# A graph and expert network on one core: pieces of 7, 14, 14, 14, groups of the second convolution moved around the carry fix, places settled inside the group's statistics

## The chip, the cores and the metric

The kernel runs on one core of a Trainium2 chip. The metric is the device time of one execution in microseconds (us). Three runs of the kernel before gave 3133.04, 3133.11 and 3134.57 us, with a median of 3133.11 us.

## The reference, cut to what matters

Two layers on 6250 nodes of 256 features: a graph attention layer with two convolutions of 8 heads by 16 channels, and a mixture of 8 experts of which each node uses two. The second convolution takes, for every edge e, the edge whose number is dst[e]. As ends are below 6250, it uses only the first 6250 edges of the list, each as many times as its number occurs among the ends, so that its sums become sums over those edges, weighted with a degree.

```python
def _gat_conv(x, W, att_src, att_dst, bias, src, dst):
    xw = (x @ W).reshape(N, H, CPH)
    a_s, a_d = einsum(xw, att_src), einsum(xw, att_dst)
    src, dst = concatenate([src, loop]), concatenate([dst, loop])
    e = leaky_relu(a_s[src] + a_d[dst], 0.2)
    m = segment_max(e, dst)
    p = exp(e - m[dst])
    alpha = p / segment_sum(p, dst)[dst]
    return segment_sum(xw[src] * alpha[:, :, None], dst).reshape(N, H * CPH) + bias

h0 = _gat_conv(x, W0, as0, ad0, b0, row, col)
h1 = _gat_conv(x, W1, as1, ad1, b1, concat([row[col], loop]), concat([col[col], loop]))
out = layernorm(concatenate([h0, h1]) + x) * gamma + beta
...
x = x + gnn(layernorm(x))
x = x + ffn(layernorm(x))     # top 2 of 8 experts, softmax of their two logits, gelu between two products
```

There are 206250 edges (200000 drawn, 6250 loops), sorted by their end `dst`.

## The kernel before, in words

The five engines (PE, DVE, ACT, POOL, SP) have an instruction stream each, written out by hand, and wait for one another on named semaphores. Nodes stand in 49 tiles of 128 (`NT`), these in 7 groups of 7 (`NG`, `GRP`).

**Projections (0 to about 170 us).** Rows of x are normalised, projected with both convolutions' weights and stored in DRAM as `tables`, one row a node: 136 numbers for each convolution (128 features and 8 source scores). Destination scores go to `adt` and are scattered to the first edge of each node (`adstart`).

**The double section (`scan_piece`, L860, L1622 to L1691).** The first 6272 edges are laid out as 128 partitions of 49 edges (`J1`). These are the edges that both convolutions use, so one gathered row of the source serves both. The 49 columns go through in four pieces, `CO` = (13, 12, 12, 12), which begin at the columns `AT`. For every column POOL issues one gather of 128 rows (L860), then DVE computes scores and scans along the columns. Scans run over a fixed width, `WA` = 14, one more than the widest piece, whatever the number of columns in the piece. ACT computes the exponentials and copies the scanned states back (`copy_piece_back`, L1090) to the buffer from which they came; SP stores them, one store for each convolution (L667). There are `NS` = 3 such buffers (slots), so the gathers of piece 3 wait for the stores of piece 0, and those of the first batch for piece 1's. Ahead of piece 0, ACT needs the scores of each partition's first node, which POOL gathers (`gather_chunk_adst`, L864) behind the gathers of piece 0.

**The batches (L880, `scan_batch`, L1699 to L1730).** The other edges are 128 partitions of 1563; they go through in 51 batches (`NB`) of 31 columns, the last of 13, over the same three slots. In batches 10 to 49 PE makes 3 or 4 columns of a batch itself by products of one-hot matrices with the table (L1332, 51 matmuls a column), and POOL gathers the other 27 or 28. The last batch has views of the width `WA` too.

**The carry fix.** Each partition begins somewhere inside a node's edges, so what the partition before it had summed must be added to one row of `state`. This is done three times: a chain of small operations (`run_maxima`, `run_sums`), a gather of the row (`gather_fix_rows`, L889), its correction (`fix_maxima`, `fix_sums`), and its store (`store_fix_rows`, L895). The third, for the last batch, lies behind all batches: POOL gathers the row once all state stores have landed, and the last states of the first convolution (`last_states1`, L910) may be gathered only once the corrected row is stored. Those of the second convolution (`last_states2`, L917) depend on neither.

**Groups.** For a group, `shares(k, g)` computes how the summed edges and the node's own loop share the weight (L1992 to L1997), ACT takes exponentials (`share_exps`), and `combine(k, g)` (L2006 to L2030) adds both to the input (`halves`); k = 0 is the first convolution and k = 1 the second. The node's own rows come by SP (`own(i)`, L684) into three buffers in the order `OWN_ORDER`; own(i) waits until the group that used the buffer is combined. Groups 0 to 3 of the second convolution are combined before the loop over groups, groups 4 to 6 in its turns 1 to 3. A turn of the loop (DVE, from L2122) is:

```python
combine(0, g)
layer_stats(halves[g], g, 0, next_shares)    # next_shares: shares(0, g + 1), and shares(1, 3 + g) in turns 1 to 3
if g >= 1:
    choose(g - 1)                            # the two best experts of the group before
if 1 <= g <= 3:
    combine(1, 3 + g)
conclude(g)                                  # gamma, add x, settle(g - 1), layer_stats(X, g, 1)
```

`layer_stats` takes means and variances (L1968, L1971), adds epsilon (L1973), releases ACT for a square root, and then computes scales (L1977, L1979), which release ACT. `settle(g - 1)` (L2060 to L2082) computes the places of the group before among its experts and releases POOL, which scatters that group's rows to `placed` (`place`, L947). After the loop DVE makes the list of tiles, and the last stage multiplies 105 tiles of 128 rows with their experts' weights (from about 2360 us); the weights are loaded by SP during the loop.

Of the kernel before, what the change touches and what calls it, by code (L numbers as in the profile page):

```python
# [28 lines left out]
P = 128  # L29
# [37 lines left out]
CO = (13, 12, 12, 12)  # L67
AT = (0, 13, 25, 37)
NA = len(CO)
WA = CO[0] + 1  # L70
# [7 lines left out]
OWN_ORDER = ((1, 0), (1, 1), (1, 2), (1, 3), (0, 0), (0, 1), (1, 4), (0, 2), (1, 5), (0, 3), (1, 6), (0, 4), (0, 5), (0, 6))  # L78
# [19 lines left out]
assert (PE1 - PE0) % 2 == 0 and CL + 1 == WA and PEC < CL and 2 * HD * WA <= HL and 2 * ROWS * WA <= ROWS * L and ZT % ZJ == 0 and ZT * P == EP  # L98
# [6 lines left out]
def build(nc, x, src, dst, W0, as0, ad0, b0, W1, as1, ad1, b1, gamma, beta, Wg, bg, eW1, eb1, eW2, eb2, out):  # L105
    ctx = ExitStack()
    with ctx:
# [474 lines left out]
        def _(sp):  # L582
            with nc.allow_non_contiguous_dma(reason="small tables, once"):
# [152 lines left out]
                for g in range(NG):  # L736
                    sp.wait_ge(conv_sum_ready, g + 1)
                    for i in ((7,), (8, 9), (10, 11), (12, 13), (), (), ())[g]:
                        own(i)
# [63 lines left out]
        def _(pool):  # L803
# [120 lines left out]
            for n in range(3):  # L924
                last_states2(n)
# [3 lines left out]
            last_states2(3)  # L929
            last_states2(4, 0, 3)  # L930
            store_fix_rows(2)
            last_states2(4, 3, 5)
# [3 lines left out]
            last_states2(4, 5, GRP)  # L936
            for n in range(2, 4):
                last_states1(n)
            last_states2(5)
# [35 lines left out]
        def _(act):  # L975
# [238 lines left out]
            share_exps(1, 1)  # L1214
            fix_exps(2)
            for g in range(2, 4):
                share_exps(1, g)
            share_exps(0, 0)
            for g in range(NG):
# [9 lines left out]
                if 1 <= g <= 3:  # L1229
                    share_exps(1, 3 + g)  # L1230
# [227 lines left out]
        def _(dve):  # L1458
# [626 lines left out]
            def conclude(g):  # L2085

                gt = slice(g * GRP, (g + 1) * GRP)
                dve.wait_ge(group_normalised, g + 1)
                V.tensor_tensor(halves[g], halves[g], bc(gam[:, :].unsqueeze(1), [P, GRP, D]), ALU.mult)
                dd()  # L2090
                dve.wait_ge(x_loaded[g], 48 if g == NG - 1 else 32)
                V.tensor_tensor(X[:, gt, :], X[:, gt, :], halves[g], ALU.add).then_inc(x_gnn_ready, 1)  # L2092
                dd()
                if g >= 1:
                    settle(g - 1)
                layer_stats(X[:, gt, :], g, 1)
# [13 lines left out]
            run_sums(2)  # L2110
            fix_maxima(2)
            combine(1, 1)
            fix_sums(2)
            shares(1, 2)
            shares(1, 3)
            combine(1, 2)
            combine(1, 3)
            shares(0, 0)
            for g in range(NG):
                combine(0, g)  # L2120

                def next_shares():  # L2122
                    if g + 1 < NG:
                        shares(0, g + 1)
                    if 1 <= g <= 3:
                        shares(1, 3 + g)
# [4 lines left out]
                if 1 <= g <= 3:  # L2131
# [147 lines left out]
```

## Time and profile before

| what | value |
|---|---|
| median of three runs | 3133.11 us |
| the profiled execution's own time | 3135.7 us |
| its span, first to last instruction | 3133.9 us |
| mean granted TensorE clock | 0.843 |
| PE busy | 2195.0 us (70%) |
| DVE busy | 2285.2 us (73%) |
| ACT busy | 1642.9 us (52%) |
| POOL busy | 1915.3 us (61%) |

A row of the timeline is the start in us from the span's beginning, the duration, the engine, the line, the operation with output and inputs, the count, and in brackets the idle time of the engine ahead of it and what ended it. Busy shares are means over stages that have different limits. POOL's gathers are 0.94 us long with 0.30 us of "issue" between two, which is not counted as busy, so POOL at 61% may have no pause at all in a stage.

### The profile page before, as it was taken

How to read it: one execution, taken by the hardware profiler on the slowest of the kernel's cores; microseconds unless marked ns; L12 is line 12 of the kernel's file. 1: busy time of each engine (PE TensorE's matmuls, PEld its weight loads, DVE VectorE, ACT ScalarE, POOL GpSimd, SP SyncE). 2: the span in 40 equal slices, each digit the busy share in tenths (PEclk: the TensorE clock that was granted, in tenths of full speed). 3: DMA queues.
4: the chain of work that ended last, by engine and by line, in shares of the span. 5: the costliest groups of instructions: out<-in, count | busy, mean ns of one | idle time of the engine just before them, and what ended most of it. 6: DMA issues, size and time to landing. Idle time of an engine off the chain costs nothing.

```text
span 3133.9 us, 45939 instructions
## 1 busy us (share of the span) xinstructions
PE 2195.0 (70%) x13176; PEld 1568.0 (50%) x13177; DVE 2285.2 (73%) x4491; ACT 1642.9 (52%) x3213; POOL 1915.3 (61%) x1901
## 2 busy tenths in 40 slices
PE   3700000068999889988998898803448999999998
PEld 1500000035555445545554554403348999999997
DVE  5667765879989999988989999877864444444443
ACT  4534444567767776777777667624333333333332
POOL 4776777777777777777777777767761222222222
PEclk8855555579999999999999999955559999999999
DMA  9445449844444444445444444464772222222222
GB/s 342 128 116 141 165 166 200 153 128 127 132 160 128 127 145 146 128 128 161 130 128 141 149 128 129 151 228 156 247 250 38 36 37 37 35 37 35 37 37 31
DMA packets 215010, 401.07 MB, mean 128 GB/s; under 512 B 78620, under 2 KB 164577, under 8 KB 208337
## 3 DMA queue, kind: packets, MB, share of 16 engines
q1 hardware_dynamic: 138721, 251.00, 24.0%
q0 software_dynamic: 75024, 147.81, 20.8%
q8 instruction: 66, 1.08, 0.1%
q14 instruction: 79, 0.65, 0.1%
q10 hardware_dynamic: 1120, 0.52, 0.1%
HBM read 207.38 MB, written 191.82 MB: 127 GB/s over the span
## 4 chain that ended last, share of the span: by engine, by line
POOL 44%; PE 25%; issue 15%; DVE 7%; DMA 2%; ACT 2%; DVEq 2%; SPq 2%; POOLq 0%; ACTq 0%
POOL AR L880 42%; PE ps L1413 12%; PE ps L1419 12%; DVE group_stats L1968 1%; ACT AR L1222 1%; DMA tables<-AR 1%; SPq L604 1%; PE ps L1404 1%; POOL adstart L840 1%; DVE AR L1728 1%; DMA state<-AR 1%; DVEq L1724 1%; SPq L588 0%; DMA AR<-tables,idx 0%; DVE AR L2092 0%
## 5 line engine op out<-in xcount | busy, mean ns | idle before, releaser
L880 POOL DMA_INDIRECT AR<-tables,idx x1423 | 1360.0, 956 | 439.8 <-issue 433.1
L956 POOL DMA_INDIRECT out<-AR,idb x105 | 186.7, 1778 | 590.6 <-issue 557.0
L1332 PE MATMUL ps<-AR,eb2b 128*128 128x408 bf16 (+1 forms) x2040 | 380.6, 352 | 165.9 <-DVE eb2b L1800 165.9
L1728 DVE TENSOR_TENSOR_SCAN AR<-ps,AR 128x512 f32<-128x512 f32 (+2 forms) x459 | 484.8, 1130 | 6.4
L1113 ACT ACTIVATE ps<-AR 128x512 f32<-128x512 f32 (+1 forms) x408 | 238.3, 592 | 345.6 <-DVE AR L1728 345.6
L1121 ACT COPY AR<-AR 128x1984 f32<-128x1984 f32 (+1 forms) x102 | 401.7, 3987 | 0.0
L1413 PEld LDWEIGHTS ps<-AR 128*128 128x128 f32 x3360 | 393.1, 193 | 6.6 <-DVE AR L2182 1.3
L1413 PE MATMUL ps<-AR 128*128 128x128 f32 x3360 | 393.7, 276 | 0.9 <-DVE AR L2182 0.9
L1332 PEld LDWEIGHTS ps<-AR,eb2b 128*128 128x128 bf16 x2040 | 206.5, 104 | 336.8 <-issue 211.0
L1332 PE MATMUL ps<-AR,scores 128*128 128x408 bf16 (+1 forms) x2040 | 349.3, 332 | 19.2 <-DVE AR L1787 19.0
L1332 PE MATMUL ps<-AR,own_pair 128*128 128x408 bf16 (+1 forms) x2100 | 352.2, 327 | 0.0
L1720 DVE TENSOR_TENSOR AR<-AR,ps 128x3968 f32<-128x3968 f32 (+1 forms) x51 | 349.3, 6848 | 1.3 <-ACT AR L1100 1.3
L2182 DVE COPY AR<-AR 128x1024 f32 x210 | 151.5, 722 | 209.8 <-PE ps L1413 208.3
L1332 PEld LDWEIGHTS ps<-AR,scores 128*128 128x128 bf16 x2040 | 195.5, 99 | 168.4 <-DVE AR L1787 24.8
L1332 PEld LDWEIGHTS ps<-AR,own_pair 128*128 128x128 bf16 x2100 | 200.4, 98 | 146.5 <-issue 0.4
L1262 ACT ACTIVATE AR<-ps,bcur 128x128 f32<-128x128 f32 x424 | 121.1, 369 | 258.4 <-PE ps L1413 258.4
L1262 ACT ACTIVATE zero<-ps,bcur 128x128 f32<-128x128 f32 x416 | 118.9, 369 | 253.5 <-PE ps L1413 253.4
L1332 PE MATMUL ps<-AR,zero 128*128 128x408 bf16 x960 | 182.1, 349 | 39.6 <-DVE AR L1787 39.6
L1162 ACT ACTIVATE scores<-AR,minus_code 128x128 bf16<-128x128 f32 x680 | 202.8, 389 | 0.0
L1349 PE MATMUL ps<-ident,sml 128*128 128x128 f32 x6 | 2.4, 502 | 278.9 <-DVE sml L1868 278.9
L1419 PE MATMUL ps<-AR 128*128 x848 | 191.9, 379 | 1.3 <-DVE AR L2225 1.3
L1419 PE MATMUL ps<-AR,zero 128*128 x832 | 188.2, 379 | 0.0
(382 smaller groups left out, 3243.2 us busy)
## 6 DMA issues: line engine op xcount, KB each, us to landing
state<-AR SPq DMA_DIRECT2D x50, 2232.0 KB
AR<-tables,idx POOLq DMA_INDIRECT x1472
AR<-in_L_ffn_W SPq DMA_DIRECT2D x16, 1024.0 KB, 9.7
AR<-placed SPq DMA_DIRECT2D x105, 130.0 KB, 2.0
adstart<-zero SPq DMA_DIRECT2D x26, 496.0 KB, 13.4
AR<-adstart SPq DMA_DIRECT2D x50, 248.0 KB, 4.3
tables<-AR SPq DMA_DIRECT2D x49, 136.0 KB, 1.9
hbd<-eb2b SPq DMA_DIRECT2D x7, 896.0 KB, 4.3
```

The source lines that it names most:

```text
L880: pool.indirect_dma_start(out=G[s][:, j, 0:ROWT], out_offset=None, in_=table_rows, in_offset=bass.IndirectOffsetOnAxis(ap=idx[:, s, j:j + ...
L956: pool.indirect_dma_start(out=out, out_offset=bass.IndirectOffsetOnAxis(ap=idb[:, s, :], axis=0), in_=ys[:, s, :], in_offset=None, bounds_ ...
L1113: S.activation(decay_of(e, w).rearrange("p (c l) -> p c l", l=w), bc(R[:, e - 1, :].unsqueeze(1), [P, CH, w]), ACT.Exp).then_inc(decays_re ...
L1121: last = S.copy(G[s][:, 0:n, a:z], TS[:, a:z, 1:n + 1].rearrange("p f j -> p j f"))
L1162: last = S.activation(onehot[c][:, a, :], column_codes[:, slot(b), c * P:(c + 1) * P], ACT.Abs, bias=minus_code[:, a:a + 1])
L1262: last = S.activation(hsT[s][:, m, :], ps[2 * s + h][:, (m % 4) * P:(m % 4 + 1) * P], ACT.Gelu, bias=bcur[:, s, m:m + 1])
L1332: mm = T.matmul(ps[n % 2][:, 0:z], mark, table_parts[k][:, a * w:a * w + z], start=(a == 0 and k == 0), stop=(a == LEV - 2 and k == PARTS ...
L1413: mm = T.matmul(ps[2 * s + h][:, m * P:(m + 1) * P], w1_cur[:, k, (h * 4 + m) * P:(h * 4 + m + 1) * P], xsT[:, s, k, :], start=(k == 0), s ...
L1419: mm = T.matmul(ps[5][:, 0:D], hsT[s][:, m, :], AR[:, bass.ds(e * (MH * D) + (NEX * KD * HID + m * D), D)], start=(m == 0), stop=(m == MH ...
L1720: V.tensor_tensor(TS[:, 0:F, js].rearrange("p (h c) j -> p h c j", h=HD), rows_in[:, :, 0:F].rearrange("p j (h c) -> p h c j", h=HD), bc(W ...
L1728: V.tensor_tensor_scan(T2[:, a:z], decay_of(e, w), T2[:, a:z], 0.0, ALU.mult, ALU.add).then_inc(entry_used, 1)
L2182: V.tensor_copy(w1_cur[:, :, h * 512:(h + 1) * 512], w1s[:, bass.ds(e, 1), :, h * 512:(h + 1) * 512].rearrange("p a k h -> p (a k) h")).th ...
```

## The change

It has three parts. The pieces of the double section have 7, 14, 14 and 14 columns, so that `WA` becomes 15. On POOL, DVE, ACT and SP the second convolution's groups are reordered around the third carry fix: POOL gathers the last states of group 3 ahead of the fix row and all of group 4 ahead of the row's store, DVE computes shares(1, 2) ahead of `fix_maxima(2)`, and combines group 4 ahead of the loop instead of in turn 1; `OWN_ORDER` follows. And `settle(g - 1)` is called inside `layer_stats(X, g, 1)`, between the variances and the wait for their square roots.

```diff
-CO = (13, 12, 12, 12)
-AT = (0, 13, 25, 37)
+CO = (7, 14, 14, 14)
+AT = (0, 7, 21, 35)
 NA = len(CO)
-WA = CO[0] + 1
+WA = max(CO) + 1
...
-OWN_ORDER = ((1, 0), (1, 1), (1, 2), (1, 3), (0, 0), (0, 1), (1, 4), (0, 2), (1, 5), (0, 3), (1, 6), (0, 4), (0, 5), (0, 6))
+OWN_ORDER = ((1, 0), (1, 1), (1, 2), (1, 3), (1, 4), (0, 0), (0, 1), (0, 2), (1, 5), (0, 3), (1, 6), (0, 4), (0, 5), (0, 6))
...
-                    for i in ((7,), (8, 9), (10, 11), (12, 13), (), (), ())[g]:
+                    for i in ((7, 8), (9,), (10, 11), (12, 13), (), (), ())[g]:
                         own(i)
...
-            for n in range(3):
+            for n in range(4):
                 last_states2(n)
             for s in range(NS):
                 pool.wait_ge(batch_stored[s], stored_count(s))
             gather_fix_rows(2)
-            last_states2(3)
-            last_states2(4, 0, 3)
+            last_states2(4)
             store_fix_rows(2)
-            last_states2(4, 3, 5)
+            last_states2(5, 0, 2)
             pool.wait_ge(fix_rows_stored, 48)
             for n in range(2):
                 last_states1(n)
-            last_states2(4, 5, GRP)
+            last_states2(5, 2, GRP)
             for n in range(2, 4):
                 last_states1(n)
-            last_states2(5)
             last_states2(6)
...
             share_exps(1, 1)
+            share_exps(1, 2)
             fix_exps(2)
-            for g in range(2, 4):
-                share_exps(1, g)
+            share_exps(1, 3)
+            share_exps(1, 4)
             share_exps(0, 0)
...
-                if 1 <= g <= 3:
+                if 2 <= g <= 3:
                     share_exps(1, 3 + g)
...
                 V.tensor_tensor(X[:, gt, :], X[:, gt, :], halves[g], ALU.add).then_inc(x_gnn_ready, 1)
                 dd()
-                if g >= 1:
-                    settle(g - 1)
-                layer_stats(X[:, gt, :], g, 1)
+
+                def settle_the_last():
+                    if g >= 1:
+                        settle(g - 1)
+
+                layer_stats(X[:, gt, :], g, 1, settle_the_last)
...
             run_sums(2)
+            shares(1, 2)
             fix_maxima(2)
             combine(1, 1)
             fix_sums(2)
-            shares(1, 2)
             shares(1, 3)
             combine(1, 2)
+            shares(1, 4)
             combine(1, 3)
+            combine(1, 4)
             shares(0, 0)
...
-                    if 1 <= g <= 3:
+                    if 2 <= g <= 3:
                         shares(1, 3 + g)
...
-                if 1 <= g <= 3:
+                if 2 <= g <= 3:
                     combine(1, 3 + g)
                 conclude(g)
```

On POOL, around the fix row's gather (L889) and its store (L895), the difference reads as follows; `eb2b`, `zero` and `hT` hold last states of the second convolution, `AR` at L910 those of the first, and x7 is one group.

```order
 L917 DMA eb2b<-state,node_index 128x144 x14
 L917 DMA zero<-state,node_index 128x144 x7
+L917 DMA hT<-state,node_index 128x144 x7
 L889 DMA fix_row<-state,fix_index 128x144
-L917 DMA hT<-state,node_index 128x144 x7
-L917 DMA eb2b<-state,node_index 128x144 x3
+L917 DMA eb2b<-state,node_index 128x144 x7
 L895 DMA state<-fix_row,fix_index 206336x144
 L917 DMA eb2b<-state,node_index 128x144 x2
 L910 DMA AR<-state,node_index 128x144 x14
-L917 DMA eb2b<-state,node_index 128x144 x2
+L917 DMA eb2b<-state,node_index 128x144 x5
```

Seven gathers went ahead of the fix row's gather, and seven instead of ten stand between it and the row's store.

On DVE, at the end of what comes ahead of the loop, the combining of group 3 was followed at once by the shares of the first convolution's group 0 (L1992 with `AR`):

```order
L2023 TENSOR_TENSOR hT<-hT,share_of 128x7x128
L2023 TENSOR_TENSOR own_pair<-own_pair,share_of 128x7x128
L2028 TENSOR_TENSOR AR<-AR,hT 128x7x128
L2030 TENSOR_TENSOR AR<-AR,own_pair 128x7x128
L1992 TENSOR_TENSOR share_of<-AR,bare 128x56
L1994 TENSOR_TENSOR share_of<-share_of,own_score 128x56
```

In the change, where these lines are numbered one less:

```order
L2027 TENSOR_TENSOR AR<-AR,hT 128x7x128
L2029 TENSOR_TENSOR AR<-AR,own_pair 128x7x128
L2005 TENSOR_TENSOR share_of<-eb2b,share_of 128x56
L2010 SCALAR_TENSOR_TENSOR share_of<-share_of 128x56
L2012 RECIPROCAL share_of<-share_of 128x56
L2014 TENSOR_TENSOR share_of<-share_of 128x56
L2018 SCALAR_TENSOR_TENSOR share_of<-share_of 128x56
L2022 TENSOR_TENSOR eb2b<-eb2b,share_of 128x7x128
L2022 TENSOR_TENSOR own_pair<-own_pair,share_of 128x7x128
L2027 TENSOR_TENSOR AR<-AR,eb2b 128x7x128
L2029 TENSOR_TENSOR AR<-AR,own_pair 128x7x128
L1991 TENSOR_TENSOR share_of<-AR,bare 128x56
```

Group 4's nine instructions of `combine` now stand there, and are gone from turn 1 of the loop.

On DVE, in the second half of a turn of the loop, the places (to L2082) came ahead of the statistics:

```order
L2074 COPY AR<-nid 128x7
L2075 COPY AR<-gate_w 128x7x2
L2082 CAST ipos<-pos 128x14
L1968 BN_STATS group_stats<-AR 128x6 x7
L1971 BN_AGGR group_mv<-group_stats 128x2 x7
L1973 TENSOR_SCALAR group_mv<-group_mv 128x7
L1977 RECIPROCAL group_scale<-group_scale 128x7
```

In the change:

```order
L1972 TENSOR_SCALAR group_mv<-group_mv 128x7
L2059 TENSOR_REDUCE mask_new<-route_of 128x8
L2061 TENSOR_SCALAR gate_w<-gate_w 128x7
L2063 TENSOR_TENSOR mask_sum<-mask_sum,mask_new 128x8
L2066 RECIPROCAL gate_w<-gate_w 128x7
L2068 TENSOR_TENSOR gate_w<-gate_w 128x7
L2070 TENSOR_TENSOR route_of<-route_of,ps 128x112
L2072 TENSOR_REDUCE pos<-route_of 128x14
L2073 COPY AR<-nid 128x7
L2074 COPY AR<-gate_w 128x7x2
L2081 CAST ipos<-pos 128x14
L1976 RECIPROCAL group_scale<-group_scale 128x7
```

The ten instructions of `settle` now stand between the operation that releases ACT for the square root and the one that needs it.

## Rows read from the trace of the kernel before

**Rows 1.** The page's part 4: the chain that ended last, by engine.
```profile
POOL 44%; PE 25%; issue 15%; DVE 7%; DMA 2%; ACT 2%; DVEq 2%; SPq 2%; POOLq 0%; ACTq 0%
```

**Rows 2.** Waits over the whole span: total us, times, longest us.
```profile
POOL AR L880 <- issue: 433.1, 1421, 0.3
...
POOL AR L880 <- DMA state<-AR: 6.4, 1, 6.4
...
POOL AR L860 <- DMA state<-AR: 4.2, 1, 4.2
```

**Rows 3.** Busy time by stretch: PE, PEld, DVE, ACT, POOL, PEclk, DMA share, GB/s.
```profile
640.00:680.00 40.00, 28.33 (x151) 15.59 (x152) 30.83 (x42) 29.34 (x52) 30.25 (x33) 0.84 0.40 127
...
720.00:760.00 40.00, 37.34 (x228) 21.37 (x226) 37.73 (x46) 34.67 (x64) 30.25 (x33) 1.00 0.44 131
...
600.00:2044.00 1444.00, 1243.20 (x7140) 696.40 (x7140) 1290.90 (x1604) 1020.72 (x1694) 1092.54 (x1154) 0.94 0.44 137
```

**Rows 4.** Timeline of POOL in the double section.
```profile
171.51 0.99 POOL L860 DMA_INDIRECT AR<-tables,idx  x1 [0.30 <-issue]
...
187.83 0.94 POOL L864 DMA_INDIRECT chunk_adst<-adt,ifirst  x1 [0.30 <-issue]
...
245.43 0.94 POOL L880 DMA_INDIRECT AR<-tables,idx  x1 [6.40 <-DMA state<-AR]
```

**Rows 5.** Timeline of DVE in the double section; L1622 begins a piece.
```profile
190.98 0.38 DVE L1622 COPY ps<-same 128x208 f32<-128x208 f32 x1 [25.97 <-ACT AR L1062]
...
212.36 0.35 DVE L1622 COPY ps<-same 128x192 f32<-128x192 f32 x1
...
224.74 7.93 DVE L1685 TENSOR_TENSOR_SCAN AR<-ps,AR 128x448 f32<-128x448 f32 x8
...
233.09 0.36 DVE L1622 COPY ps<-same 128x192 f32<-128x192 f32 x1
```

**Rows 6.** Timeline of ACT: the copies of piece 1.
```profile
230.25 6.19 ACT L1090 COPY AR<-AR 128x1728 f32<-128x1728 f32 x2
```

**Rows 7.** Timeline of SP's queue: the two stores of piece 1.
```profile
236.83 0.91 SPq L667 DMA_DIRECT2D state<-AR  x2
```

**Rows 8.** Timeline of POOL around the third carry fix.
```profile
2081.50 0.98 POOL L889 DMA_INDIRECT fix_row<-state,fix_index  x1 [11.36 <-DMA state<-AR]
...
2096.26 1.01 POOL L895 DMA_INDIRECT state<-fix_row,fix_index  x1 [0.30 <-issue]
```

**Rows 9.** DMA queues from 2070 to 2082 us: packets, MB, share of 16 engines.
```profile
q1 hardware_dynamic: 2046, 4.47, 100.7%
```

**Rows 10.** Timeline of DVE from the corrected row to the loop.
```profile
2095.17 0.06 DVE L1921 MEMSET sml<- 128x1 f32 x1
...
2096.86 0.21 DVE L2006 TENSOR_TENSOR share_of<-zero,share_of 128x56 f32<-128x56 f32 x1
...
2102.95 0.22 DVE L2006 TENSOR_TENSOR share_of<-hT,share_of 128x56 f32<-128x56 f32 x1
...
2116.18 0.22 DVE L1992 TENSOR_TENSOR share_of<-AR,bare 128x56 f32<-128x56 f32 x1 [7.23 <-DMA AR<-state,node_index]
```

**Rows 11.** Timeline of DVE in the loop; L2006 with AR begins turns 3, 4, 5.
```profile
2206.68 0.21 DVE L2006 TENSOR_TENSOR share_of<-AR,share_of 128x56 f32<-128x56 f32 x1
...
2235.90 2.39 DVE L1968 BATCH_NORM_STATS2 group_stats<-AR 128x6 f32<-128x256 f32 x7
...
2239.01 0.17 DVE L1973 TENSOR_SCALAR group_mv<-group_mv 128x7 f32<-128x7 f32 x1
2239.46 0.20 DVE L1977 RECIPROCAL group_scale<-group_scale 128x7 f32<-128x7 f32 x1 [0.27 <-ACT group_scale L1209]
...
2239.82 0.21 DVE L2006 TENSOR_TENSOR share_of<-AR,share_of 128x56 f32<-128x56 f32 x1
...
2264.39 0.21 DVE L2006 TENSOR_TENSOR share_of<-AR,share_of 128x56 f32<-128x56 f32 x1
```

**Rows 12.** Timeline of POOL: the first scatter of the last group's rows.
```profile
2332.59 0.96 POOL L947 DMA_INDIRECT placed<-AR,ipos  x1 [6.14 <-DVE ipos L2082]
```

More of the change, by code:

```diff
@@ L97 @@
 assert NBLK * BLK == E and NG * GRP == NT and (NB + NA) % NS == 1 and sum(CO) == J1 and max(CO) * 2 * ROWS <= J * ROWS
-assert (PE1 - PE0) % 2 == 0 and CL + 1 == WA and PEC < CL and 2 * HD * WA <= HL and 2 * ROWS * WA <= ROWS * L and ZT % ZJ == 0 and ZT * P == EP
+assert (PE1 - PE0) % 2 == 0 and CL + 1 <= WA and PEC < CL and 2 * HD * WA <= HL and 2 * ROWS * WA <= ROWS * L and ZT % ZJ == 0 and ZT * P == EP
 def bc(ap, shape):
```

## The prediction

> **What bounds the kernel now.** I read the chain that ended last first [rows 1]: POOL 44%, PE 25%, issue 15%. "Issue" is mostly POOL's too, the 0.30 us between two gathers. The list of waits says whether POOL ever pauses [rows 2]: its 1423 gathers of the batches have 433.1 us of issue in pieces of at most 0.3 us, and one wait of 6.4 us for a store of states; the double section's have one of 4.2 us. Both are in the double section. From its first batch gather at 245.43 us [rows 4] POOL issues one every 1.25 us until about 2044 us, never waiting. The row of that stretch agrees [rows 3]: over 600 to 2044 us POOL has 1092.5 us busy and the rest is issue, while DVE is busy 1290.9 of 1444 us and PE 1243.2. So whatever starts the batches earlier arrives whole at their end. Then come two other limits: DVE waits 7.23 us for the last states of the first convolution [rows 10], and in the loop over groups DVE is nearly always busy. The last stage is PE's and is not touched.
>
> **Part 1, the pieces.** From 171.51 to 187.83 us POOL issues 13 gathers [rows 4], 1.255 us each. With 7 columns in piece 0 the gather for the first nodes' scores comes 6 x 1.255 = 7.5 us earlier, and DVE, which waits for ACT's copy of it, starts piece 0 at 190.98 - 7.5 = 183.5 us [rows 5]. A piece of 13 columns takes DVE 212.36 - 190.98 = 21.38 us, one of 12 takes 20.73 [rows 5]: 0.65 a column. The width goes from 14 to 15, so the scans of 448 elements (7.93 us) become 480, +0.57, and I add 0.1 for the narrower full-width operations. Piece 0 then takes 20.73 - 5 x 0.65 + 0.67 = 18.2 us, and those of 14 take 22.7. Piece 0 ends at 201.6 and piece 1 at 224.3.
>
> Piece 0's stores are half as large as now and start near 203 us. POOL wants their slot after 35 column gathers and 2 for scores, at 171.5 + 37 x 1.255 = 217.9, so the wait of 4.2 us goes. What is late next is piece 1's store, which now has 14 columns. ACT's copy starts 233.09 - 230.25 = 2.8 us ahead of DVE's end and takes 6.19 us for 12 columns [rows 6], 7.2 for 14: it ends at 228.6. From the end of that copy now (236.44) to POOL's restart (245.43) are 9.0 us, the stores being issued at 236.83 [rows 7]. Two more columns in two stores are 0.29 MB, 0.8 us at the 373 GB/s that the hardware queue moved when it was full [rows 9]. POOL restarts at 228.6 + 9.8 = 238.4, having been free since 171.5 + 51 x 1.255 + 0.3 = 235.8. **Gain 245.4 - 238.4 = 7.0 us.** Bounds: only the first pause goes, 3.9 us; both go, 10.0. I take the sum, since every step of it is a row of the same code. Later slots are covered: batch 1 needs piece 2's store, about 23 us after piece 1's, and asks for it after 31 gathers, 39 us.
>
> The last batch has the width 15 too: some 140 more scan elements at 7.93 / (8 x 448) = 2.2 ns. **Cost 0.3 us** (0.1 to 0.5).
>
> **Part 2, the order around the fix.** POOL stands 11.36 us ahead of the fix row's gather, waiting for the last store [rows 8]. The seven gathers moved there take 8.8 us, so the wait hides them, and 2.6 us stay. Behind the gather the seven of group 4 wait for combine(1, 0), which ends about when the fix gather goes out, and run till about 2092.5, earlier than the corrected row at 2095.17 [rows 10]. POOL now reaches the store 1.1 us after that [rows 8] and would then wait for it, so the store leaves up to 1.0 us earlier. The two gathers behind it and the fourteen of the first convolution are as many as before, as is the traffic of SP. shares(1, 2) falls into DVE's wait for the fix row and costs nothing.
>
> The Trainium skill speaks against this move. Row first: from 2070 to 2082 us the hardware queue, which carries the last store of states, is busy 100.7% [rows 9]. "DMA: Bandwidth & Descriptors", section "Queues, rings and completion order", says that each DMA engine takes turns between the queues that have work for it. By it the moved gathers, 7 x 128 x 576 B = 0.52 MB, push that store back by their own time, and the sum would be smaller by the figure of the first rival below; by the row alone, the store lands as it does now.
>
> DVE now begins combine(1, 2) at 2096.86 and combine(1, 3) at 2102.95, 6.09 us each, and then waits 7.23 us [rows 10]. The change puts combine(1, 4) there: DVE is ready at 2116.18 - 7.23 + 6.09 = 2115.0, and the data comes at 2116.2 or up to 1.0 earlier. I take **gain 0.5 us** (from 1.1 gained to 2.5 lost). If the cover were gone, combine would cost its 6.09.
>
> In the loop, turn 3 (with a group of the second convolution) takes 2239.82 - 2206.68 = 33.1 us, and turn 4 (without) 2264.39 - 2239.82 = 24.6 [rows 11]. The 8.6 us are combine, shares, and a wait for ACT's exponentials. Turn 1 becomes one of the second kind. **Gain 8.6 us** (7.5 to 9.4). Loads of own rows change their order on SP; each still leaves at least one combine ahead of its use, and costs nothing.
>
> **Part 3, settle.** Between the variances (L1973) and the scales (L1977) DVE spends 0.45 us, 0.27 of it idle for the square root [rows 11]. With settle in between, the root is ready and only an issue gap is left. ACT gets the scales by as much earlier, and nothing is added to DVE. The six turns from 1 on give **6 x 0.36 = 2.2 us** (0.27 to 0.45 each: 1.6 to 2.7). The places are known later by the statistics, 2239.01 - 2235.90 = 3.1 us. POOL waits 6.14 us for the last group's places [rows 12], which come from behind the loop and do not get later; the group before may eat 3.1 of it. Cost zero, up to 1.5 if the weights' last loads, released by that group's scatters, press on the tile loads.
>
> **The sum:** 7.0 - 0.3 + 0.5 + 8.6 + 2.2 = **18.0 us**. Against the profiled execution's own 3135.7 us (span 3133.9) that is 3117.7; it was 2.6 us above the median of 3133.1, to which the same gain gives **3115.1 us**. A measurement of this kernel can tell about 0.2%, 6.3 us, from no change.
>
> **Rivals.**
> 1. *The store is late, and the gap overfilled.* The moved gathers delay the last store by 0.52 MB / 373 GB/s = 1.4 us, and everything behind it on the way to the corrected row; combine(1, 1), in that path, stays where it is. Gain 0.5 turns into a loss of 1.4, and up to 2.5 with a slow gather: 3117 to 3118. For it: the full queue [rows 9]. Against it: the fix row's own gather then meets less traffic. It is the page's rule above that would make this so. Chance 0.15.
> 2. *The pause only moves.* Piece 1 waits for its gathers, or its larger stores take longer, and of part 1 only the 3.9 us of the first pause remain: 3118. Against it: its last gather leaves at 199 us, 4 us before DVE wants it. Chance 0.07.
> 3. *The loop is held by the scatters.* POOL scatters a group in 14 x (0.96 + 0.30) = 18 us [rows 12] in turns of 24.6, but the late places and shorter turns bunch it up. If POOL or the weights' loads hold the end, the 10.8 us of the loop shrink to 3 and less: 3123 to 3128. Against: 6.14 us of pause at the end [rows 12]. Chance 0.05.
> 4. *Slower.* In the columns that PE makes, its clock falls at times to the lower of its levels (1.2 and 2.4 GHz): granted 0.84 over 640 to 680 us, after DVE and PE had waited for each other, 1.00 over 720 to 760 [rows 3]. At full clock a matmul there takes 37.34 / 228 = 0.164 us. A batch has 3.5 columns of 51, so 29 us, against 27.5 x 1.25 = 34 us of POOL. At the lower level it is 58, 24 us over POOL. If the shifted start lines up PE's pauses so that one whole batch more runs at the lower level, the gain is gone and more; two give 3115 + 48 = 3163. It decides from one batch and a quarter, 18 + 6.3 = 24.3. For it: the clock does dip, mean 0.94. Against: nothing in that stage moves with respect to anything else. Chance 0.04, half of it slower by 0.2%.
>
>    The Trainium skill's page "TensorE: Matmul & The Clock Gate", section "HAM oscillation — how this bites in real kernels", has waits between groups of matmuls throttle the clock again; the row with 0.84 agrees.
>
> That settle brings nothing, because what ends the wait is something else, would give 3117 and is inside the range.
>
> **The numbers.** Main case 0.69 and rivals 0.15, 0.07, 0.05, 0.04. The bounds of the parts add up to 9 to 23 us of gain. The range is 3110 to 3122: 3110 is every part at its best, and 3122 is rivals 1 and 2 together with a poor part 3. Faster by over 0.2% are the main case, rivals 1 and 2 and half of 3: 0.93. Within 0.2%: 0.05. Slower: 0.02.
>
> **What would show it.** In the new profile POOL waits for stores of the double section only ahead of the first L880, for 2 to 3.5 us, and that L880 starts near 238.4 us; L860 has no such wait. The fix row's gather goes out about 7 us earlier than 2081.5, after 2 to 4 us of pause instead of 11.4. DVE's wait ahead of the first L1991 with `AR` is under 1.5 us. Turn 1 takes 24 to 25 us and turns 2 and 3 33. The waits of L1976 for ACT's root vanish in turns 1 to 6 of the second statistics. It is wrong if the first L880 starts after 241 us, if the fix row's gather leaves less than 5 us earlier, or if the last stage, from the first tile's load on, changes its length.

## The result, and the profile after

The changed kernel takes 3116.61 us (median of 6 runs, 3115.36 to 3119.34) against 3134.62 us (6 runs, 3133.04 to 3134.92): ratio 0.9946, 95% interval 0.9935 to 0.9957, 18.0 us less. The forecast was 3115.1, range 3110 to 3122. Its profiled execution took 3115.67 us with a span of 3113.9, against 3135.7 and 3133.9 before. So this pair of profiles shows 20.0 us; 1.6 of them had come about ahead of the first L860 (169.94 us, 171.51 before), where nothing was changed.

The page's part 4 of the changed kernel, the chain by engine, answers to [rows 1]. It has hardly moved:

```profile
POOL 46%; PE 25%; issue 16%; DVE 6%; DMA 3%; ACT 2%; SPq 2%; DVEq 2%; POOLq 0%; ACTq 0%
```

The list of POOL's and DVE's waits in the changed kernel (total us, times, longest us) answers to [rows 2, 8, 10]:

```profile
POOL AR L880 <- issue: 433.0, 1421, 0.3
...
POOL placed L945 <- DVE ipos L2081: 13.8, 5, 3.7
...
POOL AR L880 <- DMA state<-AR: 3.2, 1, 3.2
POOL state L895 <- DVE sml L1920: 2.6, 1, 2.6
POOL fix_row L889 <- DMA state<-AR: 2.6, 1, 2.6
```

```profile
DVE AR L1903 <- DMA fix_row<-state,fix_index: 3.1, 1, 3.1
...
DVE share_of L1991 <- DMA AR<-state,node_index: 2.1, 1, 2.1
...
DVE AR L2027 <- DMA AR<-hbd: 1.2, 1, 1.2
...
DVE group_scale L1976 <- ACT group_scale L1207: 0.5, 2, 0.3
```

Gone are the wait of L860, 8.8 of the 11.4 us ahead of the fix row's gather, and six of the eight short waits for ACT's root. Left is one wait of 3.2 us at L880. POOL's wait of 2.6 us for the corrected row (L895) is new and was expected. New as well is a wait of 2.1 us for last states of the first convolution. The prediction had only the one ahead of the loop in mind, and that one is gone: this is another.

The double section in the changed kernel, in the order DVE, ACT, SP's queue, POOL, one fence each; compare [rows 4 to 7]:

```profile
181.54 0.28 DVE L1621 COPY ps<-same 128x112 f32<-128x112 f32 x1 [17.31 <-ACT AR L1060]
```

```profile
219.43 7.12 ACT L1088 COPY AR<-AR 128x2016 f32<-128x2016 f32 x2
```

```profile
226.94 0.91 SPq L667 DMA_DIRECT2D state<-AR  x2
```

```profile
236.62 0.94 POOL L880 DMA_INDIRECT AR<-tables,idx  x1 [3.20 <-DMA state<-AR]
```

Each stretch shows what it is worth on its own. Lengths in us, all between starts of instructions in the timelines; the runs e7 to e12 are told below.

| stretch | before | changed | e6 again | e7 pieces | e8 order | e9 settle | e10 states first | e11 settle back | e12 both mends |
|---|---|---|---|---|---|---|---|---|---|
| A first L860 to first L880 | 73.92 | 66.68 | 67.16 | 66.72 | 73.84 | 73.74 | 66.86 | 67.06 | 64.15 |
| B first to last L880 | 1797.5 | 1796.6 | 1798.9 | 1796.0 | 1800.5 | 1796.4 | 1799.0 | 1796.7 | 1794.9 |
| C last L880 to the last store of states (SP) | 27.92 | 27.64 | 30.20 | 28.63 | 27.62 | 29.16 | 27.80 | 27.79 | 27.96 |
| D that store to the fix row's gather | 10.61 | 11.71 | 11.57 | 10.39 | 12.05 | 10.30 | 11.61 | 11.74 | 11.47 |
| E fix row's gather to turn 0 of the loop | 35.97 | 34.57 | 34.82 | 36.22 | 35.47 | 36.04 | 34.63 | 34.51 | 34.54 |
| F turn 0 to the last choice (first L2036, or L2035) | 205.61 | 195.88 | 196.17 | 205.70 | 196.48 | 205.09 | 193.78 | 196.55 | 193.75 |

The 20.0 us of the first pair are 1.6 ahead of A, 7.2 in A, 0.9 in B, 0.3 in C, 0.3 in D and E together, and 9.7 in F. From the last choice to the end there are 810.8 and 810.9 us.

In F one stretch went against the rest. Turn 5, from L2005 with `AR` of the one turn to that of the next, took 24.45 us before and takes 26.12 now. DVE and POOL in the changed kernel:

```profile
2243.15 0.21 DVE L2005 TENSOR_TENSOR share_of<-AR,share_of 128x56 f32<-128x56 f32 x1
...
2254.65 0.22 DVE L1991 TENSOR_TENSOR share_of<-AR,bare 128x56 f32<-128x56 f32 x1 [2.07 <-DMA AR<-state,node_index]
...
2269.27 0.21 DVE L2005 TENSOR_TENSOR share_of<-AR,share_of 128x56 f32<-128x56 f32 x1
```

```profile
2218.88 0.99 POOL L945 DMA_INDIRECT placed<-AR,ipos  x1 [2.09 <-DVE ipos L2081]
...
2238.67 0.96 POOL L945 DMA_INDIRECT placed<-AR,ipos  x1 [0.30 <-issue]
2239.93 0.99 POOL L910 DMA_INDIRECT AR<-state,node_index  x1 [0.30 <-issue]
...
2249.10 0.94 POOL L910 DMA_INDIRECT AR<-state,node_index  x1 [0.30 <-issue]
```

`shares(0, 6)` needs the last states of group 6. POOL gathers them (L910, until 2249.10) behind the 14 scatters of group 2, which it could begin only when that group's places were known, at 2218.88. In the kernel before, POOL's last gather for group 6 stood at 2264.44, and DVE wanted it at 2273.67, 9.2 us later; here these are 2249.10 and 2252.6 (2254.65 - 2.07), and the data takes 5.6:

```profile
2264.44 0.98 POOL L910 DMA_INDIRECT AR<-state,node_index  x1 [0.30 <-issue]
```

```profile
2273.67 0.26 DVE L1992 TENSOR_TENSOR share_of<-AR,bare 128x56 f32<-128x56 f32 x1
```

The margin before was therefore 9.24 - 5.55 = 3.7 us. My theory when the experiments began: the places that settle now gives 3.1 us later, and the turn that became shorter, used it up together.

### The profile page after: what moved, and what is told of

It is laid out like the page before. It is cut to its first block, busy times and chain, and to the rows that moved or that the text cites. A ratio compares the mean times of both kernels' runs of the same rounds, so it can differ in the third digit from the quotient of the medians.

```text
span 3113.9 us, 45939 instructions
## 1 busy us (share of the span) xinstructions
PE 2202.4 (71%) x13176; PEld 1572.2 (50%) x13177; DVE 2287.4 (73%) x4491; ACT 1644.8 (53%) x3213; POOL 1920.0 (62%) x1901
## 4 chain that ended last, share of the span: by engine, by line
POOL 46%; PE 25%; issue 16%; DVE 6%; DMA 3%; ACT 2%; SPq 2%; DVEq 2%; POOLq 0%; ACTq 0%
POOL AR L880 43%; PE ps L1412 12%; PE ps L1418 12%; POOL adstart L840 1%; DMA tables<-AR 1%; PE ps L1403 1%; DVE group_stats L1967 1%; ACT AR L1221 1%; DMA state<-AR 1%; SPq L604 1%; POOL placed L945 1%; SPq L588 0%; DVE AR L1684 0%; DVE AR L2091 0%; DVE AR L2088 0%
## 5 line engine op out<-in xcount | busy, mean ns | idle before, releaser
L880 POOL DMA_INDIRECT AR<-tables,idx x1423 | 1359.1, 955 | 436.5 <-issue 433.0
L1331 PE MATMUL ps<-AR,zero 128*128 128x408 bf16 x960 | 188.5, 357 | 39.0 <-DVE AR L1786 39.0
```

The lines of the kernel that those rows point to most:

```text
L880: pool.indirect_dma_start(out=G[s][:, j, 0:ROWT], out_offset=None, in_=table_rows, in_offset=bass.IndirectOffsetOnAxis(ap=idx[:, s, j:j + ...
L1331: mm = T.matmul(ps[n % 2][:, 0:z], mark, table_parts[k][:, a * w:a * w + z], start=(a == 0 and k == 0), stop=(a == LEV - 2 and k == PARTS ...
```

## The experiments

### Five runs on chips where the kernel takes 4400 us

The first five runs went to two chips on which the kernel before takes 4416.9 us (e1 to e4) and 4378.7 us (e5), not 3134. Of their expectations only the fifth allows for that.

e1, the pieces alone:

```diff
-CO = (13, 12, 12, 12)
-AT = (0, 13, 25, 37)
-WA = CO[0] + 1
+CO = (7, 14, 14, 14)
+AT = (0, 7, 21, 35)
+WA = max(CO) + 1
```

> The kernel before with the pieces of 7, 14, 14, 14 alone. My theory: the pieces are worth what the two traces show, 7.2 us at the first L880 counted from the first L860 (73.9 us before, 66.7 us expected), less 0.3 us for the wider last batch, and it all arrives: 6.5 to 7.5 us faster than before. It arrives whole because POOL never waits between that L880 and the last batch. Rival A (the pause only moves): the first L880 comes 3.9 us earlier, 3 to 4 us in the time. Rival B: the gain is eaten where POOL's stream ends, since the last store, PE's columns or DVE's scan are what the last batch waits for, and less than half of the shift at L880 is seen at the fix row's gather. The last store of states, with only three groups of gathers beside it as before, should take 10.6 us from SP's issue to POOL's restart (it took 11.7 in the changed kernel with seven more gathers beside it).

e2, the order alone: the change without this and without the move of settle.

> The kernel before with the new order around the fix alone (POOL, DVE, ACT and SP lists), pieces and settle as before. My theory: the first L880 stays at 245 us; turn 1 of the loop falls from 33.5 to 24 us (9.6) and the gap before the first shares of the first convolution gains about 1, less nothing later, as the places are not late here: 9.5 to 10.5 us faster than before. Rival A (my first rival in the prediction, the overfilled gap): the seven more gathers push the last store back by 1.4 us, the gap loses 1 to 2, and the gain is 7 to 8 us. Rival B: the wait of 2 us for the last states of group 6 comes from the shorter loop alone, not from the late places, and shows here too ahead of the sixth turn's shares: 8 us faster. By my theory that wait is under 0.5 us here.

e3, settle alone:

```diff
-                if g >= 1:
-                    settle(g - 1)
-                layer_stats(X[:, gt, :], g, 1)
+                def settle_the_last():
+                    if g >= 1:
+                        settle(g - 1)
+
+                layer_stats(X[:, gt, :], g, 1, settle_the_last)
```

> The kernel before with settle between the variances and the scales, nothing else. My theory: in the kernel before POOL has slack in the loop (turns 1 to 3 long), so the late places cost nothing and the six closed gaps are seen: 2.2 us faster (1.6 to 2.7). Rival A: something else ends the turns, 0 us. Rival B: the places 3.1 us later hold POOL back here too, a wait of about 2 us for the last states of group 6 shows, and the time is the same or up to 1 us worse.

e4, POOL's order alone: the piece of the diff around `gather_fix_rows(2)`, and nothing on DVE, ACT and SP.

> The kernel before with POOL's new order alone: the fourth group of seven gathers moved ahead of the fix row's gather, DVE, ACT and SP as before, so that turn 1 still holds group 4 of the second convolution. My theory: the moved gathers only fill a wait; 0.5 to 1.5 us faster than before, and what the new order brings comes from DVE's side, the turn made short. Rival: POOL's chain was what held the loop, and moving its gathers alone brings 5 us or more.

e5, the changed kernel with POOL's loop written in another order:

```diff
             for n in range(NG):
+                if n == 2:
+                    last_states1(n + 4)
                 place(n)
-                if n + 4 < NG:
+                if n < 2:
                     last_states1(n + 4)
```

> The changed kernel with one thing moved on POOL: the last states of the first convolution's group 6 are gathered ahead of the scatters of group 2, not behind them. My theory: in the changed kernel the sixth turn of the loop is 1.7 us longer than before the change because DVE waits 2.07 us for these states, and they are late because POOL waits 2 to 4 us for places in three turns and then scatters 18 us first. Moved ahead, they are there in time: the wait ahead of the sixth turn's shares vanishes, that turn takes 24.1 instead of 26.1 us, and the kernel takes 1.5 to 2.5 us less than the changed one (20 less than the kernel before). Rival A: the scatters of group 2, then 9 us later, make the wait move to POOL's next places and to the last group's, 0 us or up to 2 worse. Rival B: DVE's wait there is for something else, and it stays. On a chip where the kernel before takes 4417 us, as in the four runs ahead of this one, the loop is held by something else (POOL waits 9 to 18 us for places in every turn) and all three expect 0.

Measured, as ratios to the kernel before on the same chip: e1 0.9976 (0.9936 to 1.0016), e2 0.9958 (0.9920 to 0.9996), e3 0.9965 (0.9932 to 0.9998), e4 0.9962 (0.9930 to 0.9994), e5 0.9993 (0.9958 to 1.0028). The medians are 4420.4, 4403.8, 4413.2 and 4412.8 us, and 4369.1 for e5; as plain ratios 1.0008, 0.9970, 0.9991, 0.9991 and 0.9978. The intervals of e2, e3 and e4 end just below 1, but the two ways to take a ratio differ by up to 0.3%, as much as the effects, and half a width of 0.3 to 0.4% is 14 to 18 us: e1 to e5 decide nothing between their theories. e4, POOL's order alone, was not run again on another chip, so what POOL's list brings without DVE's is not known. The profile says why the five could not decide. POOL's waits in e1:

```profile
POOL AR L880 <- DMA state<-AR: 1127.4, 23, 59.7
```

Busy time from 1070 to 1080 us in e1, then in the changed kernel on the first chip (PE, PEld, DVE, ACT, POOL, PEclk, DMA share, GB/s), both in the columns that PE makes while POOL gathers:

```profile
1070.00:1080.00 10.00, 1.99 (x4) 0.31 (x3) 0.00 (x0) 0.00 (x0) 7.57 (x8) 0.50 0.39 118
```

```profile
1070.00:1080.00 10.00, 10.00 (x62) 5.74 (x61) 9.71 (x9) 8.15 (x19) 7.56 (x9) 1.00 0.25 57
```

And PE in e1, where the bracket is its idle time before the matmul:

```profile
1073.33 0.50 PE L1332 MATMUL ps<-AR,scores 128*128 128x408 bf16 x1 [1.61 <-issue]
1076.12 0.50 PE L1332 MATMUL ps<-AR,scores 128*128 128x408 bf16 x1 [2.29 <-issue]
...
1117.45 3.92 PE L1332 MATMUL ps<-AR,scores 128*128 128x408 bf16 x11 [0.20 <-issue]
```

PE issues one matmul in 1.4 to 2.8 us (once in 4.2), where the first chip makes 62 in 10 us. In this batch it begins 11 us after POOL has taken up its gathers (1040.07 us) and ends 5 us after its last one (about 1108 us). PE and POOL so work by turns: POOL waits up to 59.7 us for a slot. The batches are not POOL's alone there, and the prediction's "whatever starts the batches earlier arrives whole at their end" does not hold.

It is not PE alone. This is DVE in piece 1 of the double section in e1, while PE does nothing at all:

```profile
239.50 0.39 DVE L1622 COPY ps<-same 128x224 f32<-128x224 f32 x1
...
260.16 0.45 DVE L1664 TENSOR_TENSOR AR<-AR,ps 128x112 f32<-128x112 f32 x2 [4.75 <-issue]
...
283.65 0.39 DVE L1622 COPY ps<-same 128x224 f32<-128x224 f32 x1
```

The piece takes 44.2 us and not the 22.5 of the first chip. DVE is busy 21.52 us in both; here eleven pauses put down to "issue", 22.5 us in all, stand between its instructions, and the last of them ends as POOL makes its last gather of the section (267.86 us). POOL then waits 27.8 us for that piece's store. That is most of why stretch A is longer there, and why it changes its sign: 91.5 us in e1 with the new pieces, 87.7, 87.5 and 87.9 in e2 to e4 with the old ones. In e2 the pauses of that piece are 13.6 us and POOL's waits 4.3 and 20.2.

In the loop of e5 POOL waits 4.6 to 11.8 us for places in every turn, and DVE waits for no last states, so POOL's gathers hold nobody. Why these chips do this is open; no run tried it.

### The change again, and its three parts, at 3136 us

The sixth run was the changed kernel itself.

> The changed kernel itself, once more. If this chip runs the kernel before in 3134 us, as where the change was first measured: 18 us faster. If it runs it in 4380 to 4420 us, as the chips of the five runs ahead of this one, my theory (there PE issues one matmul in 1.4 to 2.8 us for as long as POOL gathers, so POOL and PE work by turns and the stream of batches is no longer POOL's alone) expects that the first L880 comes 3 to 4 us later than with pieces of 13, 12, 12, 12 (91.5 us from the first L860 in the run with the pieces alone, 87.5 to 87.9 in the three without them), and that the time is 5 to 15 us less than before, from the loop alone. Rival: the gain of 18 us holds wherever the kernel runs, since the loop and the double section have nothing to do with the batches.

It came to a chip with 3136.2 us for the kernel before, and the changed kernel took 3122.76 (3122.08 to 3123.30): ratio 0.9953 (0.9937 to 0.9970), 13.4 us. Stretches A and F are those of the first profile within 0.5 us. Its profiled span is 7.7 us longer (3121.6); 1.6 of that stand ahead of A and 4.9 in B and C, where the table has scatter of that size between profiles. "The gain is 18" is thus good to some 3 us, though each mechanism is good to half a microsecond. Runs e7 to e10 then went to the same chip (12), with 3137.64 us for the kernel before.

e7, the pieces alone again.

> The kernel before with the pieces of 7, 14, 14, 14 alone, once more, on a chip that runs the kernel before in 3135 us. My theory: the first L880 starts 66.7 us after the first L860 (73.9 before) and 6.5 to 7.5 us arrive in the time. Rival A (the pause only moves): 3 to 4 us. The last store of states takes 10.6 us from SP's issue to POOL's restart, as before and not 11.7 as in the changed kernel, if the seven gathers beside it are what delayed it there. On a chip that takes 4400 us: the first L880 3 to 4 us later than before, no change in the time.

3131.27 us, ratio 0.9981 (0.9972 to 0.9991), 6.4 us less. POOL in this kernel:

```profile
238.40 0.94 POOL L880 DMA_INDIRECT AR<-tables,idx  x1 [3.23 <-DMA state<-AR]
...
2073.41 0.94 POOL L889 DMA_INDIRECT fix_row<-state,fix_index  x1 [11.83 <-DMA state<-AR]
```

A is 66.72 us, 7.2 less than before; the rival with 3 to 4 us is out. D is 10.39 us, as in the two other profiles with the old order (10.61, 10.30).

e8, the order alone again.

> The kernel before with the new order around the fix alone, once more. My theory: 9.5 to 10.5 us faster than before: turn 1 of the loop 33.5 to 24 us, the gap before the loop about 1 better, and no wait above 0.5 us for the last states of group 6, since the places are not late here. Rival A (the overfilled gap): 7 to 8 us. Rival B (the shorter loop alone makes that wait of 2 us): 8 us, and the wait shows. On a chip that takes 4400 us: 5 to 15 us faster.

3127.88 us, ratio 0.9971 (0.9959 to 0.9983), 9.8 us less. POOL in this kernel, then DVE at the last shares before the loop:

```profile
2084.98 1.01 POOL L889 DMA_INDIRECT fix_row<-state,fix_index  x1 [3.18 <-DMA state<-AR]
...
2099.44 1.07 POOL L895 DMA_INDIRECT state<-fix_row,fix_index  x1 [3.74 <-DVE sml L1920]
```

```profile
2119.15 0.22 DVE L1991 TENSOR_TENSOR share_of<-AR,bare 128x56 f32<-128x56 f32 x1 [0.72 <-DMA AR<-state,node_index]
```

F is 9.1 us shorter, all of it in turn 1 (33.50 to 24.36 us). DVE still waits 0.72 us, so the gap is filled and not overfilled. But D is 12.05 us: the first rival's mechanism is real. E is half a microsecond shorter than before, which does not make up for it: D and E together are 47.5 us against 46.6, so the gap, expected about 1 us better, is 0.9 worse. By the stretches this run gains 9.1 - 0.9 = 8.2 us, which is rival A's figure (7 to 8) and not my theory's; the median of 9.8 can't decide, as the stream of batches scatters by more than the difference. There is no wait for group 6's last states, so the short turn alone does not cause it.

e9, settle alone again.

> The kernel before with settle between the variances and the scales, nothing else, once more. My theory: POOL has slack in that kernel's loop, so 2.2 us faster (1.6 to 2.7). Rival A: something else ends the turns, 0 us. Rival B: the later places cost here too, a wait of about 2 us for the last states of group 6, and 0 to 1 us slower.

3136.77 us, ratio 0.9999 (0.9989 to 1.0009): nothing. My theory missed here, and the wait of Rival B came:

```profile
2273.88 0.22 DVE L1992 TENSOR_TENSOR share_of<-AR,bare 128x56 f32<-128x56 f32 x1 [2.04 <-DMA AR<-state,node_index]
```

Turns 1 to 4 are 33.10, 32.96, 32.76 and 24.10 us, 0.4 to 0.5 less each than in e7 (33.57, 33.39, 33.13, 24.57), and turn 5 is 26.10 against 24.43. So the late places are enough by themselves, and POOL's slack in the kernel before was smaller than I took it for.

e10, the kernel of e5 again.

> The changed kernel with the last states of group 6 gathered ahead of the scatters of group 2 on POOL, once more. My theory: DVE's wait of 2.07 us ahead of the sixth turn's shares vanishes, that turn takes 24.1 and not 26.1 us, and the kernel takes 1.5 to 2.5 us less than the changed one: 20 less than the kernel before where the changed one gives 18, 15.5 where it gives 13.4 as in the run ahead of this one. Rival A: the scatters of groups 2 and on come 9 us later and hold the last places, 0 to 2 us worse than the changed one. Rival B: the wait stays.

3118.62 us, ratio 0.9942 (0.9925 to 0.9960), 19.0 us less. DVE no longer waits at these shares (L1993 in this kernel), as the missing bracket says:

```profile
2255.72 0.21 DVE L1993 TENSOR_TENSOR share_of<-AR,bare 128x56 f32<-128x56 f32 x1
```

Turn 5 takes 23.90 us, F 193.78: 2.1 to 2.4 us less than the changed kernel. No later wait of POOL for places is longer than before: 2.03 and 2.59 us ahead of the last two groups, as in the changed kernel. The expectation of 15.5 us was short: Of the 6.2 us between its profile and that of e6, 2.4 are F, and nearly all of the rest is again C and what comes ahead of A.

### Two last runs

They went to a chip (4) with 3134.45 us for the kernel before. e11 is the changed kernel with the diff of e3 undone: `settle` stands ahead of the statistics again, as in the kernel before. ("Behind the scales" in the expectation is a slip.)

> The changed kernel with settle put back behind the scales. My theory, after the run with settle alone: the move closes gaps of 0.27 us and more in every turn (2.2 us in all) and gives the same 2 us back as DVE's wait for the last states of group 6, because it makes the places 3.1 us later and POOL scatters before it gathers. Put back, turns 1 to 4 are 0.4 us longer each, the sixth turn 24.5 us without that wait, and from the loop's first turn to the last choice it takes 196.3 to 196.7 us, against 195.9 and 196.2 in the two profiles of the changed kernel: the same time within 0.5 us. Rival: the move is worth its 2.2 us and the wait comes from the shorter loop, so that the wait stays and the kernel is 2 us slower than the changed one. On a chip that takes 4400 us: no difference can be told.

3117.61 us, ratio 0.9947 (0.9933 to 0.9961): the changed kernel's own 0.9946. F is 196.55 us, within the 196.3 to 196.7 expected, and `shares(0, 6)` does not wait:

```profile
2254.56 0.25 DVE L1991 TENSOR_TENSOR share_of<-AR,bare 128x56 f32<-128x56 f32 x1
```

e12 is e10 with smaller first and larger last pieces:

```diff
-CO = (7, 14, 14, 14)
-AT = (0, 7, 21, 35)
+CO = (5, 14, 15, 15)
+AT = (0, 5, 19, 34)
```

> The changed kernel with two mends: the last states of group 6 ahead of the scatters of group 2, as in the run before, and pieces of 5, 14, 15, 15 columns (width 16). My theory of part 1: what is left there is POOL's wait of 3.2 to 3.5 us for piece 1's store; a first piece of 5 lets DVE begin 2.5 us earlier, each wider piece costs it 0.6 us, and the first L880 starts 64.0 to 64.5 us after the first L860 (66.7 to 67.2 with 7, 14, 14, 14), after a wait of 0.3 to 1.2 us. Less 0.3 us for the last batch, 2 us less than with the first mend alone: 21 us faster than the kernel before, ratio 0.9935. Rival A: the wider pieces make a later store late (a wait in batch 1 or 2), and nothing or less is gained. Rival B: POOL's stream is not what starts the batches any more, the 2.5 us do not arrive at the end. On a chip that takes 4400 us: nothing can be told.

3113.40 us (3110.96 to 3114.85), ratio 0.9933 (0.9919 to 0.9947), 21.05 us less than before. POOL now reaches the first batch without a wait for a store:

```profile
235.43 0.94 POOL L880 DMA_INDIRECT AR<-tables,idx  x1 [0.54 <-issue]
```

A is 64.15 us, inside 64.0 to 64.5, and F is 193.75. It is the fastest of all that ran. That it beats the changed kernel rests on A (2.5 us, in this one profile) and F (2.1, here and in e10); the intervals of the two ratios overlap.

## Why the prediction was right, point by point

**The double section** was right in each step. DVE begins piece 0 at 181.54 us, 11.6 us behind the first L860; the prediction had 183.5 - 171.5 = 12.0. Piece 0 takes 18.4 us (18.2 predicted), piece 1 22.5 (22.7), ACT's copy 7.1 (7.2). From its end, 226.55 us, to POOL's restart are 10.1 us (9.8). Gain 7.2 against 7.0, and 6.4 us of it in the time of e7. The last batch's 0.3 us can't be told: C is 27.6 to 29.2 us with the old width and 27.6 to 30.2 with the new one.

**The gap around the fix** came out near its sum where the new pieces ran with it (D and E: 46.58 us before, 46.28 and 46.39 in the changed kernel; 0.5 predicted), but not in e8, and a step of it was wrong. "By the row alone, the store lands as it does now" failed. With seven more gathers beside it the last store lands after 11.5 to 12.1 us (six profiles), without them after 10.3 to 10.6 (three): 1.3 us, where the rival had worked out 1.4. SP's transfers ahead of that store are the same in all of them. The delay agrees with what the Trainium skill's page "DMA: Bandwidth & Descriptors", section "Queues, rings and completion order", says, that a DMA engine takes turns between its queues. Other loads pay as well: DVE waits 0.7 to 1.6 us for `hbd` with the new order, at most 0.3 with the old.

What made good for it is E, 1.2 to 1.5 us shorter in the five profiles that have the new pieces too. Before, it ended with a wait for data [rows 10]; now it ends with DVE's own work, from the corrected row to the first shares:

```profile
2085.74 0.06 DVE L1920 MEMSET sml<- 128x1 f32 x1
...
2105.87 0.22 DVE L1991 TENSOR_TENSOR share_of<-AR,bare 128x56 f32<-128x56 f32 x1
```

These are 20.1 us without a pause. The states are no longer late because POOL's first L910 starts 17.9 us behind the fix row's gather and not 19.1: 0.7 us come from the corrected row's store, which POOL issues 14.0 us behind the gather and not 14.8 [rows 8], and 0.5 from one L917 behind that store, which took 0.96 us and not 1.50. In e8 that L917 took 1.81 us, the first L910 stands at 19.2, DVE waits 0.7 us, and the gap as a whole loses 0.9. The half microsecond predicted here thus hangs on how long single gathers take, which the prediction had in its bounds (2.5 us lost "with a slow gather") but not in its sum.

**Turn 1** was mis-sized by little: 8.6 predicted, from the difference of turns 3 and 4; e8 shows 9.1 (33.50 to 24.36).

**Settle** was right in its mechanism and size: without the new wait it is worth 2.8 us in F (196.55 in e11, 193.78 in e10; 2.2 predicted). The step that failed is "Cost zero". I had weighed the 3.1 us by which places come later against POOL's pause ahead of the last group's scatters [rows 12], and that pause was the wrong cover. Behind `place(2)` in POOL's program stand the last states of group 6, and their margin was 3.7 us. Seen from the start of turn 4, POOL begins those scatters 3.6 us later than before (at 2218.88, with the turn's start at 2219.05; before at 2236.09, with the start at 2239.82), its way through them and the gathers takes 30.2 us and not 28.4, and DVE wants the states 0.3 us earlier in the turn: 5.8 in all, 2.1 more than the margin. So 2 us were given back, and settle brought about half a microsecond (F is 0.5 us shorter in e9 than before, and 0.4 and 0.7 shorter in the two profiles of the changed kernel than in e11).

Of the signs it named, all came but a small one: turn 1 takes 23.9 us, just under the 24 to 25. (The waits of L1976 in the second statistics of turns 1 to 6 are all gone; the two left are that of turn 0, where nothing is settled, and one in the first statistics of turn 6.) In sum: 7.2 + 0.3 + 9.1 + 0.5 = 17.1 us from the parts' own stretches, 6.37 + 9.76 + 0.87 = 17.0 us from the medians of e7, e8 and e9, 18.0 and 13.4 measured for the whole. Taken from the ratios, the three parts give 15.4 us and the whole 16.9 and 14.7. The forecast of 18.0 had settle almost 2 us too high and turn 1 half a microsecond too low. Its closeness is in good part luck: the stream of batches scatters by more than that, and the same kernel gained 13.4 us on another chip.

Of the rivals, the first came with its late store in all six profiles of the new order, and with a loss for the whole gap only in e8. The second (the pause only moves) and the third (loop held by the scatters, 7.8 us less) are refuted as told; the third was right in kind, since POOL's order in the loop did hold DVE once, for 2 us. The fourth did not occur on the chips with 3134 to 3138 us, where stretch B (1795 to 1800.5 us) and the mean granted clock of the profiles (0.842 to 0.846) hardly move. On the two with 4400 us PE was held up, not by the clock alone but by its issue, with old pieces and new ones alike; the kernel before was timed there, but not profiled.

## What to carry to other kernels

When a result is moved to a later place, look its cost up at everything that stands behind its consumer in that queue, not only at the consumer's own next pause. Here 14 scatters stood ahead of 7 gathers whose data had a margin of 3.7 us, and moving the gathers ahead gave the 2 us back.

In this pipeline a small first piece paid, since what waits for it starts earlier, at the price of wider later ones. Work out when each store must have landed, and stop where the issuing engine no longer waits (5, 14, 15, 15 here).

Filling a wait for a transfer with other transfers is nearly free, but not quite: seven gathers of 0.52 MB in total delayed the awaited store by 1.3 us.

## What the runs showed of the hardware

On two of the chips that ran these kernels, engines issued their instructions late while POOL issued gathers. TensorE issued one matmul in 1.4 to 2.8 us (2.3 us idle between matmuls of 0.50 us, granted clock 0.50, the lower level of 1.2 GHz), from about 11 us after POOL took up its gathers until about 5 us after its last, against 0.16 us a matmul on the others. DVE had 22.5 us of such pauses in one piece in which it was busy 21.5 us, against none. The whole kernel took 4379 to 4417 us in place of 3134 to 3138. There the pieces of 7, 14, 14, 14 lose 3.6 to 4.0 us in the double section, which they shorten by 7.2 elsewhere. A tuning of a few microseconds holds for the chips on which it was measured.

Among chips with the usual time, the same stream of 1423 gathers (stretch B) took 1795 to 1800.5 us from profile to profile, and this, with C (27.6 to 30.2 us) and what comes ahead of A (169.6 to 171.7), makes most of the scatter between profiles.

In each of six profiles (the kernel before, the changed kernel, e6, e8, e9, e12) 35 to 40 of the 1570 gathers of 128 rows took 1.1 to 2.7 us, and nearly all others 0.94 to 1.0. Behind the corrected row's store one of them took 0.96 us in the changed kernel, where DVE then did not wait, and 1.81 us in e8, where it waited 0.7 us.
